# Routed rows in one running layout, with eight quad units and six shared batches put first

## The reference

```python
logits = jnp.einsum('bsh,eh->bse', x, router_w) + routing_bias
probs = jax.nn.sigmoid(logits)
scores, indices = jax.lax.top_k(probs, 2)                 # two of 8 experts for each token
scores = scores / jnp.sum(scores, axis=-1, keepdims=True)
w = w.at[jnp.arange(t)[:, None], idx].add(sc)
g = jax.nn.silu(jnp.einsum('th,ehi->tei', xf, gate_w))    # I = 256
u = jnp.einsum('th,ehi->tei', xf, up_w)
combined = jnp.einsum('tei,eih,te->th', g * u, down_w, w)
return shared + combined                                   # shared: the same network with its own weights, for all tokens
```

## Time and profile before

| | us |
|---|---|
| median of three runs | 706.74 (706.07 to 708.89) |
| the profiled execution | 704.36 |
| its span, first to last instruction | 702.6 |
| PE busy | 638.1 (91%) |
| DVE busy | 538.8 (77%) |
| ACT busy | 456.4 (65%) |
| POOL busy | 307.8 (44%) |

### The profile page before, as it was taken

The page is one execution under the profiler, slowest core; times in us unless marked ns, Lnnn a source line. Parts: engine busy times, 40 slices in busy tenths (PEclk is TensorE's granted clock), DMA queues, the critical chain, the costliest instruction groups (busy, mean ns, idle before and its releaser), DMA issues.

```text
span 702.6 us, 16427 instructions
## 1 busy us (share of the span) xinstructions
PE 638.1 (91%) x5432; PEld 402.7 (57%) x5432; DVE 538.8 (77%) x1903; ACT 456.4 (65%) x816; POOL 307.8 (44%) x511
## 2 busy tenths in 40 slices
PE   7489999999999999998999999999986788898983
PEld 7255555555555555554455555555565577786653
DVE  5799877798788878799878877878257745576886
ACT  3367776767767768776677866776745545565651
POOL 4393631323133223223478422422664276546673
PEclk9699999999999999999999999999999999999996
DMA  9200543621121112211241110211553376794424
GB/s 253 68 1 3 158 133 110 176 86 47 51 77 46 35 33 84 55 56 39 58 133 65 54 52 17 57 38 41 118 119 107 83 133 129 146 176 91 113 58 131
DMA packets 102768, 60.24 MB, mean 86 GB/s; under 512 B 44568, under 2 KB 94640, under 8 KB 102688
## 3 DMA queue, kind: packets, MB, share of 16 engines
q1 hardware_dynamic: 66144, 28.22, 16.7%
q10 hardware_dynamic: 32336, 22.29, 11.1%
q0 software_dynamic: 4208, 8.69, 4.8%
HBM read 19.62 MB, written 30.77 MB: 72 GB/s over the span
## 4 chain that ended last, share of the span: by engine, by line
PE 73%; DVE 11%; issue 5%; ACT 4%; another core or an unknown queue 1%; POOL 1%; ACTq 0%; DVEq 0%; POOLq 0%
PE bank L1058 9%; PE bank L1037 9%; PE bank L1075 9%; PE bank L1060 8%; PE bank L1059 8%; PE bank L998 4%; PE bank L1166 4%; PE bank L1000 4%; PE bank L999 4%; PE bank L1164 3%; PE bank L1165 3%; DVE junk L1455 2%; PE bank L1202 2%; PE bank L1204 2%; PE bank L1203 2%
## 5 line engine op out<-in xcount | busy, mean ns | idle before, releaser
L1327 ACT ACTIVATE p_sb<-bank,inv_scale 128x512 f32<-128x512 f32 (+1 forms) x384 | 222.1, 614 | 43.2 <-PE bank L1060 35.0
L1455 DVE CUSTOM_DVE_ANT_0 junk<-bank,causal 128x512 bf16<-128x512 f32 (+3 forms) x512 | 222.0, 483 | 29.0 <-PE bank L1037 27.5
L931 POOL TENSOR_SCALAR_AFFINE_SELECT p_sb<-p_sb 128x384 f32<-128x384 f32 x128 | 66.8, 522 | 280.3 <-ACT p_sb L1327 279.4
L1059 PE MATMUL bank<-ql,ah 128*128 128x512 f16 (+3 forms) x512 | 153.1, 299 | 0.0
L1060 PE MATMUL bank<-qh,al 128*128 128x512 f16 (+3 forms) x512 | 152.7, 299 | 0.0
L1058 PE MATMUL bank<-qh,ah 128*128 128x512 f16 (+3 forms) x512 | 146.9, 300 | 0.3 <-ACT p_sb L1327 0.3
L1037 PE MATMUL bank<-ah,qh 128*128 128x512 f16 (+3 forms) x512 | 130.1, 300 | 1.2 <-DVE low L1455 1.2
L1427 DVE TENSOR_TENSOR ql<-bank,qh 128x512 f16<-128x512 f32 x128 | 88.3, 690 | 42.8 <-ACT qh L1292 40.5
L1292 ACT ACTIVATE qh<-bank 128x512 f16<-128x512 f32 x128 | 76.4, 597 | 34.4 <-PE bank L1000 33.0
L1639 DVE SCALAR_TENSOR_TENSOR al<-bank,gu_scale,ah 128x512 f32<-128x512 f32 x69 | 51.6, 748 | 59.5 <-ACT ah L1358 43.1
L978 POOL DMA_INDIRECT p_sb<-ys_dram,place x64 | 67.9, 1061 | 39.6 <-PE bank L1166 17.4
(11 more groups left out here) (246 smaller groups left out, 1127.0 us busy)
## 6 DMA issues: line engine op xcount, KB each, us to landing
o_dram<-oT ACTq DMA_DIRECT2D x32, 256.0 KB, 2.3
ys_dram<-ql ACTq DMA_DIRECT2D x25, 256.0 KB
xs_dram<-causal ACTq DMA_DIRECT2D x6, 832.0 KB, 4.5
wst<-in_Wkqv SPq DMA_DIRECT2D x8, 264.0 KB, 5.0
x_sb<-in_x SPq DMA_DIRECT2D x8, 256.0 KB, 6.1
out<-x_sb SPq DMA_DIRECT2D x8, 256.0 KB
o_all<-o_dram SPq DMA_DIRECT2D x7, 256.0 KB
r_all<-r_dram SPq DMA_DIRECT2D x7, 256.0 KB
```

Of the source, the lines that this page charges most:

```text
L1059: nc.tensor.matmul(bank, m.ah[:, keys], ql[:, s, c * P:N], start=False, stop=False)
L1327: nc.scalar.activation(p_sb[v % P_RING][:, S_AT[k]:S_AT[k] + S_WIDTH[k]], m.psum[S_BANK[k]][:, 0:S_WIDTH[k]], ACT.Exp, scale=m.inv_scale[: ...
L1455: last = nc.vector.tensor_tensor_reduce(out=junk[:, S_AT[k] + at:S_AT[k] + at + w], in0=m.psum[M_BANK[k]][:, at:at + w], in1=m.causal[:, N ...
```

## The change: what it does

1. **Four parts.** `SPLITS` becomes batches 0 to 3 (16 tiles), 4 and 5 (8), 6 (4), 7 (4). The first three share one running layout: a later part fills the room that its expert has left in tiles already opened, and opens new tiles behind. Part 3 has tensors of its own. There are 35 pairs in the running layout and 11 apart, 46 instead of 53, so 46 + 16 = 62 units and 24 quads instead of 28.
2. **A new order.** `ORDER` puts 4 quads (8 units) first, those that part 0 is sure to have filled; then the shared batches 0 to 5 (12 units), the 20 other quads (38 units), and the shared batches 7 and 6 (4 units).
3. **Later steps.** Batch 7's steps spread over slots 4 to 20 (`spread` 7, `proj` 10, `norm` 14, `late` 16, `logits` 19, `exp` 20). Batch 6's exponential no longer stands beside batch 7's but in slot 3. Part 1's sends stand in slots 0 to 10, part 2's sort in 5 to 8 and its sends in 13 to 17, part 3's sort in 21 and 22 and its sends in 28 to 32.
4. **More steps of routing.** For each part DVE also works out the excess over the room left, the new tiles, and the jump from old room to new (`base`, `slots`, `next`).
5. **Fetches.** A row of part 0 may lie in any of the first 23 pairs, so part 0's fetches wait for the first 12 quads, part 1's for 16, part 2's for 18 and part 3's for 24. `FETCH_AT` becomes slots 43, 51, 54 and 65; the spacing is 5/3 for each slot, so the planned slots run from 43 to 81, of which the loop has 70. Behind slot 62 a fetch waits for no unit.
6. Smaller tables and buffers, and registers with the experts' numbers loaded closer to their use (`load_word`).

```diff
-SPLITS = ((0, 12), (12, 24), (24, 32))
+SPLITS = ((0, 16), (16, 24), (24, 28), (28, 32))
...
+PAIRS_BY = tuple(2 * (t1 - (0 if g < APART else t0)) * P // WIDE + E - 1 for g, (t0, t1) in enumerate(SPLITS))
+SLOT_TILES = tuple(2 * n for n in PAIRS_BY[APART - 1:])
+QUADS_BY = tuple(sum(1 for k, first, _ in QUAD_TILES if k < g // APART or (k == g // APART and first < 2 * n)) for g, n in enumerate(PAIRS_BY))
...
-ORDER = ("part", 0), ("part", 1), ("part", 2), ("shared", 8)
-SHARED_ORDER = (6, 5, 0, 7, 1, 2, 3, 4)
+ORDER = ("quads", (0, FULL_QUADS)), ("shared", (0, 1, 2, 3, 4, 5)), ("quads", (FULL_QUADS, QUADS_BY[-1])), ("shared", (7, 6))
...
-FETCH_AT = tuple(FFN_AT + end + LATE + 3 for end in part_ends)
+FETCH_AT = tuple(FFN_AT + quad_ends[n - 1] + LATE + 3 for n in QUADS_BY)
...
-            x = max(x, -(-FETCH_AT[g] * 3 // 2))
-            while sends_at(x * 2 // 3):
+            x = max(x, -(-FETCH_AT[g] * 5 // 3))
+            while sends_at(x * 3 // 5):
...
-LAST_STEPS = {"gather": 1, "rinv": 2, "spread": 3, "mult": NEVER, "proj": 4, "stats": 4, "aggr": 4, "newton0": 5, "newton1": 5, "newton2": 5, "norm": 5, "late": 6, "late_copy": 7, "logits": 8, "exp": 9, "split": 10}
+LAST_STEPS = {"gather": 1, "rinv": 2, "spread": 4, "mult": NEVER, "proj": 7, "stats": 8, "aggr": 9, "newton0": 10, "newton1": 10, "newton2": 11, "norm": 11, "late": 13, "late_copy": 14, "logits": 16, "exp": 17, "split": 14}
...
                 if late_at("exp", t):
-                    for b in (B - 2, B - 1):
-                        act.wait_ge(t_taken, T_TURN["logits", b] + 1)
-                        nc.scalar.activation(ex[:, seg(b, TB), :], lg[:, b % 2, :, :], ACT.Exp, scale=-1.0).then_inc(ex_ready, 1)
+                    act.wait_ge(t_taken, T_TURN["logits", B - 1] + 1)
+                    nc.scalar.activation(ex[:, seg((B - 1) % EX_BATCHES, TB), :], lg[:, (B - 1) % 2, :, :], ACT.Exp, scale=-1.0).then_inc(ex_ready, 1)
...
+                def new_tiles(wanted, shift):
+                    c.link(nc.vector.scalar_tensor_tensor(out=above[:, :, :], in0=wanted.unsqueeze(2).to_broadcast([P, E, FULL]), scalar=shift,
+                                                          in1=m.full_tiles[:, :].unsqueeze(1).to_broadcast([P, E, FULL]), op0=ALU.add, op1=ALU.is_gt))
+                    c.link(nc.vector.tensor_reduce(out=n_tiles[:, :], in_=above[:, :, :], axis=AX.X, op=ALU.add))
+                    c.link(nc.vector.tensor_tensor(stacked[:, :, :], n_tiles[:, :].unsqueeze(1).to_broadcast([P, E, E]), m.lower_experts[:, :, :], ALU.mult))
...
+                if (g := part_at("base", t)) is not None:
+                    c.link(nc.vector.tensor_tensor(excess[:, :], counts(g), room[:, :], ALU.subtract))
+                    new_tiles(excess[:, :], 0.0)
+                    c.link(nc.vector.tensor_reduce(out=jump[:, :], in_=stacked[:, :, :], axis=AX.X, op=ALU.add))
+                    c.link(nc.vector.tensor_scalar(regions[:, g + 1, :], jump[:, :], base[:, 0:1], None, ALU.add))
+                    c.link(nc.vector.tensor_tensor(jump[:, :], regions[:, g + 1, :], room[:, :], ALU.subtract))
+                    c.link(nc.vector.tensor_tensor(jump[:, :], jump[:, :], opened(g), ALU.subtract))
...
+            def fetch_rows(t):
+                for g, i, k in fetches_at(t):
+                    if (i, k) == (SPLITS[g][0], 0):
+                        for r in range(X_RING):
+                            pool.wait_ge(ys_stored[r], 16 * stores_before(QUADS_BY[g], r))
+                        pool.wait_ge(pv_done, GROUPS)
+                    if k == 0 and t - FFN_AT <= UNITS_F:
+                        pool.wait_ge(gate_up, t - FFN_AT)
```

More of the change, by code:

```diff
@@ L563, in __init__ @@
         self.batch, self.half, self.quad, self.a, self.n, self.job = batch, half, quad, a, n, job
-        self.shared = quad is None
-        self.width = N if self.shared else n * WIDE
-        self.finishes = half == 1 if self.shared else True
-        self.first_of_job = half == 0 if self.shared else a == 0
-        self.last_of_job = half == 1 if self.shared else a + n == quad.n
-quads, units, jobs, part_begins, part_ends = [], [], [], [], []
+        self.whole = quad is None
+        self.width = N if self.whole else n * WIDE
+        self.finishes = half == 1 if self.whole else True
+        self.last_of_job = half == 1 if self.whole else a + n == quad.n
+quads, units, jobs = [], [], []
 for kind, n in ORDER:
-    if kind == "shared":
-        for _ in range(n):
-            b = SHARED_ORDER[sum(1 for job in jobs if job[0] == "shared")]
+    if kind != "quads":
+        for b in n:
             for half in range(2):
                 units.append(Unit(b, half, None, 0, 0, len(jobs)))
-            jobs.append(("shared", b))
+            jobs.append((kind, b))
     else:
-        part_begins.append(len(units))
-        for first in range(0, SLOT_TILES[n], 4):
-            quad = Quad(len(quads), n, first, min(4, SLOT_TILES[n] - first))
+        for q in range(*n):
+            quad = Quad(q, *QUAD_TILES[q])
             quads.append(quad)
@@ L596, with column_of @@
 SLOTS = FFN_AT + UNITS_F + LATE + 4
-FETCH_AT = tuple(FFN_AT + end + LATE + 3 for end in part_ends)
+FETCH_AT = tuple(FFN_AT + quad_ends[n - 1] + LATE + 3 for n in QUADS_BY)
 COMBINE_LATE = 5
+def column_of(quad, a):
+    return 2 if quad.apart else 1 if (quad.first + a) // 2 >= WORD else 0
+word_units = {}
+for u, unit in reversed(list(enumerate(units))):
+    if unit.quad:
+        word_units[column_of(unit.quad, unit.a), (unit.quad.first + unit.a) // 2 // WORD] = u
 def unit_at(u):
@@ L615, in downs_that_read, with stores_before @@
     return downs_by(u)
-def stores_before(part, k):
-    return sum(1 for quad in quads if quad.part <= part and quad.q % X_RING == k)
+def stores_before(n, k):
+    return sum(1 for q in range(n) if q % X_RING == k)
 def plan_sends():
-    slots = {}
+    slots, at = {}, 0
     for g, (t0, t1) in enumerate(SPLITS):
-        at = 6 * part_step_at("send", g)
+        at = max(at, 6 * part_step_at("send", g))
         for i in range(2 * (t1 - t0)):
@@ L666, in taken_after, with taken_by @@
 def taken_after(b):
-    return SHARED_ORDER.index(b) + 1
+    return taken_by(jobs.index(("shared", b)))
+def taken_by(job):
+    return sum(1 for kind, _ in jobs[:job + 1] if kind != "quad")
 def added_at(b):
-    return FFN_AT + LATE + 1 + next(u for u, unit in enumerate(units) if unit.shared and unit.batch == b and unit.finishes)
+    return FFN_AT + LATE + 1 + next(u for u, unit in enumerate(units) if unit.whole and unit.batch == b and unit.finishes)
 def rows_at(i):
@@ L749, in body @@
     picked = sb("picked", [P, TILES, E], F16)
-    totals = sb("totals", [P, sum(len(c) for c in CHUNKS), P], F16)
+    totals = sb("totals", [P, len(CHUNKS[0]), P], F16)
     above = sb("above", [P, E, FULL], F32)
@@ L1135, in after_attention @@
                     turn("rank", g)
-                    base = sum(len(c) for c in CHUNKS[:g])
                     rows = [(t1 - t0) * E for t0, t1 in CHUNKS[g]]
@@ L1177, in up @@
                     pe.wait_ge(gu_ready, u - DEEP + 1)
-                if unit.shared:
+                if unit.whole:
                     if unit.half == 0 and unit.batch < B - 1:
@@ L1627, in feed_forward @@
             def feed_forward(u):
-                if (unit := unit_at(u - LATE - 1)) and unit.shared and unit.finishes:
+                if (unit := unit_at(u - LATE - 1)) and unit.whole and unit.finishes:
                     b = unit.batch
```

219 lines of the change are left out of this document (127 added, 92 removed).

## The result

The changed kernel takes 742.62 us (median of four runs, 741.68 to 746.01), and four runs of the kernel before beside it 706.40 (704.88 to 708.89): a ratio of 1.0522, with a 95% interval of 1.0493 to 1.0551. The profiled execution took 742.18 us with a span of 740.4, against 704.36 and 702.6. The prediction had the direction and the first part of the reason, 716.2 us in a range of 703 to 726, but a quarter of the size: 9.5 us more were forecast, 37.8 came in the span.

A forecast was written before the change was run, and what follows sets the result against it. DVE was to bound units 5 to 29, then POOL's 64 fetches the end: last issue at 702.2 plus a 9.9 tail gives 712.1, 9.5 us over the earlier span, so 716.2 us, range 703 to 726.

The forecast's parts named there:

- DVE's work between units 5 and 29: Units, shared additions, last batch's chain and routing on DVE, 63.3 us for 24 units, more than PE's 1.98 each.
- Batch 7's exponential: Slot 20: ACT's table loads around this exponential leave DVE idle for 2.8 us.
- Rival A: Up to slot 43: DVE's steps fit into idle time, slot 43 at about 600.9, 701.6 us in all; chance 0.18.
- D's sign: A chain ending through PE, for the rival with fetches hidden by PE, some 25 us less; chance 0.02.
- The tail: From the last fetch's issue to the end of the span: landing, eight additions and store, staying at 9.9 us.
- Unit 29 to the first fetch: From unit 29 at DVE to POOL's first fetch behind slot 43: 26.5 us, PE up to two units ahead.
- Unit 5 to unit 29: Feed-forward stretch bound by DVE: 63.3 us of work plus 2.8 idle for an exponential, 66.1 us.
- The start: Unit 5 reaches DVE at 523.3: 520.3 as before plus 3.0 for batch 6's exponential, attention's extra routing taken at 0.
- rival C: Attention loses 4.5 us or unit 20 waits 4, units run at 2.39: 723 to 725 us; chance 0.16.
- the exponential in slot 3: Batch 6's exponential in its new place: table loads leave DVE idle 3.0 us, bounds nothing to 3.4.
- the two bounds for slot 43: Slot 43 at 611 with units at 1.98 us, or 619.7 at 2.39; the middle, 615.5, was taken.
- Rival B: Fetches get quicker once DVE is quiet: the last 31 at 1.25 in step, 3.7 us less, 712.5; chance 0.14.

The follow-up runs named there:

- before_late: The kernel before with no fetch planned earlier than slot 37 and six more loop slots: 721.34 us, ratio 1.0152.
- pace32: The kernel after with fetches planned 3 in 2 slots in place of 5 in 3: 734.95 us, ratio 1.0398.
- sends_wide: The kernel after with fetches planned 3 in 2 slots and six POOL clears ahead of each of the last batch's eight sends: 728.73 us, one run.
- no_table: The kernel after with batch 6's exponential made a silu, so that its two table loads go: 741.21 us, ratio 1.0474.
- dve_busy: The kernel after with 60 small idle additions on DVE just ahead of its wait for shared batch 7's `down`: 747.22 us, one run.
- before_unpaced: The kernel before with its fetches' waits on PE's units taken away: 763.75 us, ratio 1.0801.

## Why the prediction was wrong in size

**Right.** The reason for being slower at all: the removed units gave nothing, all 64 fetches start late, and the end can't come before POOL's chain is through; before_late shows the late start by itself. Also right were DVE's work between units 5 and 29 (59.0 us busy and 2.9 in gaps under 0.15 us, 61.9 in all, against 63.3) and the fetches' length (87.7 against 86.3, though by paced fetches slower and unpaced ones quicker than its 1.37 in step). Batch 7's exponential cost DVE less than forecast, 1.6 us against 2.8:

```profile
575.16 0.75 DVE L1711 SCALAR_TENSOR_TENSOR al<-bank,gu_scale,ah 128x512 f32<-128x512 f32 x1 [1.64 <-ACT ah L1389]
```

Rival A (PE sets the pace, slot 43 by 601) did not come near. Of the prediction's signs of being right three failed: PE was to be done 30 us or more before POOL's last fetch, the first fetch was to come at 613 to 620, and the fetches behind slot 62 at 1.3 to 1.4 in step (1.25). Of its signs of being wrong two came: a first feed-forward matmul later than 506 (508.4) and an end that PE decides. The latter was D's sign, but D's mechanism (fetches hidden) did not come.

**The tail, 12.1 us short.** The prediction let it "stay" at 9.9, because PE would be "off the path". That step failed: the tail measured 22.0, and PE was on the path. It is the largest single miss, though without it the time would be 730.5 and still beyond 726. It put the unpaced fetches behind slot 62 down as POOL's affair alone, and never asked who works beside them: PE's last two `down`s. Before the change each tile's fetch beside PE's last units still waited for one of them; after it 33 come at 1.25 us without a gap, from 678.4 on. Every kernel with the change in which POOL issued more slowly beside those `down`s, or not at all, has a tail of 9.9; in pace32 PE was then done 39 us before the last fetch, as forecast.

**Unit 29 to the first fetch, 3.6 short.** The crawl again, beside the last batch's sends; sends_wide gives 25.3, in one run.

**Unit 5 to unit 29, 9.0 short.** The prediction took DVE to be the bound and let it idle for the two exponentials alone. That step failed too: it idled 16.0 us, 2.9 in the small gaps of its chains, 1.6 for the exponential and 11.5 elsewhere, 9.8 of it behind ACT, which waited for PE. The forecast had counted the small gaps in its windows, so the missing term is the 11.5, less what the exponential and DVE's work came out under the forecast. Neither of the two handshakes that I took away returned it. One part was overlooked: the granted clock was 0.89 over this stretch (0.93 before the change, 520.28 to 597.29), and in some of it PE ran at its lower level, its matmuls of 256 columns 0.21 us apart in place of 0.11. The longest idle time of DVE falls there (window of all engines, then PE's and DVE's timelines):

```profile
587.00:590.00 3.00, 3.00 (x22) 2.50 (x21) 1.04 (x2) 1.69 (x3) 0.00 (x0) 0.50 0.18 41
```

```profile
587.35 0.42 PE L1195 MATMUL bank<-mh,wh 128*128 128x256 f16 x1
587.56 0.42 PE L1196 MATMUL bank<-ml,wh 128*128 128x256 f16 x1
588.96 0.75 DVE L1711 SCALAR_TENSOR_TENSOR al<-bank,gu_scale,ah 128x512 f32<-128x512 f32 x1 [2.52 <-ACT ah L1389]
```

PE was busy for only 1.9 of the 3.6 us before (583.0 to 586.6), so the clock may itself be a result of the waits; no run parts the two. With spaced sends the way from unit 0 to unit 29 was 2.7 to 5.2 us shorter (84.1 in both kernels, against 86.8 to 89.3), but the granted clock was higher too (0.93 and 0.95 from unit 5 to unit 29). So it is likely, and not shown, that the crawl is part of the term. How much is crawl, clock or handshake is open.

**The start, 2.3 late.** Unit 0 is 3.9 us late, which the prediction had in its bounds (0 to 4.5) and in rival C but took at 0. The way from there to unit 5 was 14.2 us, 1.4 more than before the change (12.7), where the prediction had 3.0 for the exponential in slot 3. That these 1.4 are the exponential's is not shown: without its table loads (no_table) the same way took 15.8. Rival C (more is lost) was thus the nearest, with 0.16, and its 725 was its own end. The range ended there because every bound in it was put on a cost that the trace of before had shown. Two slips in its working moved nothing much: of the two bounds for slot 43, 619.7 has the 0.8 us taken off by which `up` runs ahead of DVE and 611 has not; and the 39.8 us of DVE's idle time in the earlier trace rows run to 650 only, to the end they are 43.1.

**The fetches' pitch.** Rival B was right on its own point: the fetches without DVE beside them take 1.25 us in step. The gain was eaten by gaps in the paced ones. The Trainium skill ("SBUF — State Buffer", "SBUF: two separate sides") has DVE hold up the descriptors of POOL's DMAs while it runs in a mode that uses two ports. The trace agrees in direction: a fetch took 1005 ns in the mean with DVE idle beside the last 27 of 64, 1061 before. Whether DVE's instructions here use such a mode, no run shows.

The Trainium skill says on the same page ("Who interferes with whom") that a DMA never contends with a compute engine. The page says it of the ports of the SBUF, and no run here shows where the engines are held up. But beside POOL's indirect DMAs they are, with all queues at 52 GB/s together: PE's matmuls start 0.70 us apart and more, and in dve_busy so do DVE's additions.

## What to carry to other kernels

Ask of each transfer that is moved not only when it starts but at what pitch it comes and which engines issue many short instructions beside it. A wait that holds POOL's indirect DMAs to the pace of the compute engines can be worth far more than it costs (56.5 us here); plan a slower pitch than POOL's own. When one chain of transfers sets the end, count back from its first member: here PE's units behind that point were free, as long as they did not crawl. And a long wait in the list is worth what the next wait in line leaves of it; only an experiment tells.

## What the runs showed of the hardware

- POOL's indirect DMAs of 128 rows, back to back at 1.25 us, let PE (kernel after, before_unpaced) and DVE (dve_busy) start an instruction mostly only each 0.70 us or a multiple. At 1.48 us between fetches PE got through with some stalls (last shared addition at 698.4 in place of 726.5); between sends 1.50 was not enough (units 29 to 32 in 11.1 us), 2.3 to 2.6 was (5.0 us, one run).
- It isn't the amount of data: POOL's queue had 19% of the DMA engines' time from 686 to 724 and all queues together moved 52 GB/s, while in before_unpaced PE filled all of its 20 us beside 129 GB/s from other queues. Where in the chip the instructions are held up is open. No packet of an instruction queue is recorded in that stretch, and the profile shows only "issue".
- The crawl keeps itself going: PE holds up DVE, both stand still, and POOL is slowed by neither, so it stays at 1.25 until its fetches end (the last starts at 718.39, DVE's addition of PE's result at 724.49) or it has to wait.
